# Softplus of a state space layer in two halves, with the work around it moved to other steps

## The reference

```python
xz = xs @ in_proj_w.T;  xin, z = split(xz)           # 768 channels each, L = 2304 positions
xin = silu(causal depthwise conv of xin, 4 taps)
dt, Bm, Cm = split(xin @ x_proj_w.T)                 # 24, 16, 16
dt = softplus(dt @ dt_proj_w.T + dt_proj_b)          # 768 step sizes for each position
h_t = exp(dt_t * A) * h_(t-1) + dt_t * B_t * x_t     # 16 states for each channel
y_t = sum over states of h_t * C_t
y = (y + xin * D) * silu(z);  out = layernorm(y @ out_proj_w.T)
```

## Time and profile before

| | |
|---|---|
| median of 3 runs | 5353.92 us (5347.02 to 5355.37) |
| profiled execution | 5347.93 us, span 5346.1 us |
| mean granted TensorE clock | 0.962 |
| busy share of the span | PE 88%, DVE 82%, ACT 57%, POOL 56% |

### The profile page before, as it was taken

The page is one execution under the profiler, slowest core; times in us unless marked ns, Lnnn a source line. Parts: engine busy times, 40 slices in busy tenths (PEclk is TensorE's granted clock), DMA queues, the critical chain, the costliest instruction groups (busy, mean ns, idle before and its releaser), DMA issues.

```text
span 5346.1 us, 78656 instructions
## 1 busy us (share of the span) xinstructions
PE 4686.3 (88%) x28623; PEld 3835.5 (72%) x28623; DVE 4381.3 (82%) x4965; ACT 3070.4 (57%) x6391; POOL 2970.7 (56%) x3552
## 2 busy tenths in 40 slices
PE   4888888888888888888888886779998899999999
PEld 2666666666666666666666665446877799999999
DVE  1999999999999999999999999677677765665555
ACT  3777777777777777777777774333332223333333
POOL 3776777777777777777777775456554520000000
PEclk8999999999999999999999999889797988999999
DMA  2001000001000001000000001110201021112110
GB/s 78 1 13 33 10 10 10 10 11 35 10 10 10 10 11 35 10 10 10 10 10 10 10 5 44 44 32 20 92 20 41 26 72 53 54 51 60 45 60 29
DMA packets 96933, 148.64 MB, mean 28 GB/s; under 512 B 5748, under 2 KB 93604, under 8 KB 96548
## 3 DMA queue, kind: packets, MB, share of 16 engines
q1 hardware_dynamic: 96548, 143.63, 8.4%
HBM read 101.00 MB, written 42.61 MB: 27 GB/s over the span
## 4 chain that ended last, share of the span: by engine, by line
PE 50%; issue 15%; DVE 15%; POOL 12%; ACT 7%; DMA 1%; POOLq 0%; DVEq 0%; SPq 0%; ACTq 0%
PE pw L1776 8%; PE pw L1763 6%; PE pw L462 6%; PE pw L451 6%; DVE a_h L744 5%; POOL a_dBT L882 4%; PE ps L413 3%; PE ps L353 3%; DVE b_cv L1393 3%; PE ps L373 2%; DVE a_acc L763 2%; PE ps L1763 2%; POOL a_xin L834 2%; POOL a_acc L894 2%; PE pw L1176 2%
## 5 line engine op out<-in xcount | busy, mean ns | idle before, releaser
L744 DVE TENSOR_TENSOR_SCAN a_h<-a_dA,pw 128x771 f32<-128x771 f32 x1152 | 2015.7, 1752 | 125.6 <-PE pw L451 124.6
L600 ACT ACTIVATE a_dA<-a_dt,a_Aneg 128x384 f32<-128x384 f32 x2304 | 1345.5, 607 | 155.0 <-DVE a_h L744 150.1
L462 PEld LDWEIGHTS pw<-g_ident,a_h 128*128 128x128 f32 x6912 | 786.6, 142 | 619.8 <-DVE a_acc L763 267.1
L882 POOL TENSOR_SCALAR a_dBT<-a_dtxT,a_BC 128x768 f32<-128x768 f32 x1152 | 1026.2, 909 | 300.7 <-PE pw L451 216.6
L462 PE MATMUL pw<-g_ident,a_h 128*128 128x128 f32 x6912 | 983.1, 279 | 227.5 <-DVE a_acc L763 158.1
L451 PE MATMUL pw<-g_ident,a_dBT 128*128 128x128 f32 x6912 | 958.9, 276 | 4.8 <-POOL a_dBT L882 4.8
L763 DVE SCALAR_TENSOR_TENSOR a_acc<-pw,a_BC,a_acc 128x768 f32<-128x768 f32 x912 | 915.3, 1004 | 52.5 <-PE pw L462 48.1
L451 PEld LDWEIGHTS pw<-g_ident,a_dBT 128*128 128x128 f32 x6912 | 806.5, 143 | 6.5 <-POOL a_dBT L882 5.5
L834 POOL TENSOR_TENSOR a_xin<-a_xin,a_tm 128x384 f32<-128x384 f32 x432 | 433.3, 1003 | 34.2 <-ACT a_tm L521 9.0
L1887 DVE TENSOR_TENSOR d_hf<-d_hf,d_wb 128x384 f32<-128x384 f32 x288 | 159.1, 557 | 312.4 <-ACT d_hf L1819 300.2
L894 POOL TENSOR_TENSOR a_acc<-a_acc,a_tm 128x768 f32<-128x768 f32 x168 | 307.4, 1830 | 171.1 <-ACT a_tm L614 170.2
(11 more groups left out here) (228 smaller groups left out, 9377.7 us busy)
## 6 DMA issues: line engine op xcount, KB each, us to landing
d_wb<-cw SPq DMA_DIRECT2D x24, 768.0 KB, 5.7
a_xs<-in_x SPq DMA_DIRECT2D x24, 576.0 KB, 3.9
x<-a_xs SPq DMA_DIRECT2D x24, 576.0 KB, 3.0
b_x<-x SPq DMA_DIRECT2D x24, 576.0 KB, 4.4
b_xs<-x SPq DMA_DIRECT2D x24, 576.0 KB, 5.0
e_xs<-x SPq DMA_DIRECT2D x24, 576.0 KB, 3.8
out<-e_xs SPq DMA_DIRECT2D x24, 576.0 KB, 5.8
a_sx<-in_x SPq DMA_DIRECT2D x54, 192.0 KB, 2.3
```

Of the source, the lines that this page charges most:

```text
L462: t = e.transpose(m["pw2"][:, c * 128:(c + 1) * 128], m[f"a_h{g % 2}"][:, c // 2, first_col(c) + tb * 128:first_col(c) + (tb + 1) * 128], ...
L600: e.activation(dA[:, first_col(c):first_col(c) + T], m[f"a_dt{k % 2}"][:, c, :], ACT.Exp, scale=m["a_Aneg"][:, c, n:n + 1]).then_inc(s["a_ ...
L744: e.tensor_tensor_scan(m[f"a_h{g % 2}"][:, p % 3, :], m[f"a_dA{pi % NDA}"][:], m[f"pw{pi % 2}"][:, COL:COL + PAIR], 1.0, ALU.mult, ALU.add ...
L882: t = e.tensor_scalar(m[f"a_dBT{g % 2}"][:, tb, :], m[f"a_dtxT{o}"][:, tb, :], m[f"a_BC{o}"][:, tb, n:n + 1], 1.0, ALU.mult, ALU.mult)
```

## The change

The softplus is taken in two halves of three channel tiles: ACT does V0 to V2, Exp and Ln of these, then V3 to V5, Exp and Ln of those, and POOL starts on the first three when their Ln is done. PE issues V3 to V5 two steps later, G2 two steps later, T0 to T5 some 3 to 5 steps earlier, and Z0 to Z5 0.6 to 5.7 steps later. The bank named by `V_BANK` is ps3 for all six, as before, so `pi` is `ps`.

```diff
@@ -310,9 +310,12 @@
 
 A_AT = (6.2, 8, 9.8, 11.6, 13.4, 15.2)
 O_AT, O_GAP, LN_AT = (18.8, 30, 40.2), (1.8, 1.6, 1.1), (29.5, 39.8, 47)
-G_AT = (60, 62.5, 66)
-T_AT = (78.6, 79.8, 81, 85.6, 86.6, 87.6)
-Z_AT = (63.5, 67.5, 71.5, 75, 82, 88.8)
+G_AT = (60, 62.5, 68)
+T_AT = (74, 75, 76, 82.4, 83.4, 84.4)
+V_BANK = "SSSSSS"
+SP_AT = (61, 66.5)
+DT_AT = (64.5, 66.5, 68.5, 70.5, 72.5, 74.5)
+Z_AT = (65.6, 69.6, 77.2, 79, 85.6, 89.4)
 
 LENT = (20, 22, 24, 26, 38, 41, 43)
 
@@ -387,7 +390,7 @@
         t = e.transpose(ps[:, tb * 32:tb * 32 + 32], m["a_tm0"][32:64, tb * 128:(tb + 1) * 128], ident[32:64, 32:64])
     t.then_inc(s["pe_BC"], 1)
     for i in range(6):
-        yield 58 + 0.8 * i
+        yield 58 + 0.8 * i + 2 * (i // 3)
         S.claim("a_v", 6 * k + i + 1)
         w.wait_ge("v_dt3", k + 1)
         w.wait_ge("v_w", 7)
@@ -537,23 +540,26 @@
     w.wait_ge("p_dbt", NS * (k - 1))
     e.activation(m[f"a_BC{o}"][:], ps[:, 0:96].rearrange("p (a n) -> p a n", n=32), ACT.Copy).then_inc(s["a_bc"], 1)
     dt = m[f"a_dt{o}"]
-    for i in range(6):
-        yield 58.4 + 0.8 * i
-        w.wait_ge("pe_V", 6 * k + i + 1)
-        w.wait_ge("p_cv", 24 * (k + 1))
-        if k % NQ < NQ - 1:
-            w.wait_ge("p_halo", k + 2)
-        w.wait_ge("p_dtx", 6 * (k - 1))
-        w.wait_ge("a_exp", 3 * PAIRS * (k - 1))
-        e.activation(dt[:, i, :], ps[:, 0:T], ACT.Abs, bias=pv[:, i, 5:6])
-        e.activation(raw[:, i, 3:T + 3], ps[:, 0:T], ACT.Relu, bias=pv[:, i, 5:6]).then_inc(s["a_v"], 1)
-    yield 64.5
-    w.wait_ge("a_v", 6 * (k + 1))
-    e.activation(dt[:], dt[:], ACT.Exp, scale=-1.0).then_inc(s["a_sp"], 1)
-    yield 67
-    w.wait_ge("a_sp", 2 * k + 1)
-    w.wait_ge("p_const", 3)
-    e.activation(dt[:], dt[:], ACT.Ln, bias=m["a_one"][:, 0:1]).then_inc(s["a_sp"], 1)
+    for hf in range(2):
+        for i in range(3 * hf, 3 * hf + 3):
+            yield 58.4 + 0.8 * i + (2 if hf else 0)
+            pi = ps if V_BANK[i] == "S" else pd
+            w.wait_ge("pe_V", 6 * k + i + 1)
+            w.wait_ge("p_cv", 24 * (k + 1))
+            if k % NQ < NQ - 1:
+                w.wait_ge("p_halo", k + 2)
+            w.wait_ge("p_dtx", 6 * (k - 1))
+            w.wait_ge("a_exp", 3 * PAIRS * (k - 1))
+            e.activation(dt[:, i, :], pi[:, 0:T], ACT.Abs, bias=pv[:, i, 5:6])
+            e.activation(raw[:, i, 3:T + 3], pi[:, 0:T], ACT.Relu, bias=pv[:, i, 5:6]).then_inc(s["a_v"], 1)
+        half = dt[:, 3 * hf:3 * hf + 3, :]
+        yield SP_AT[hf]
+        w.wait_ge("a_v", 6 * k + 3 * hf + 3)
+        e.activation(half, half, ACT.Exp, scale=-1.0).then_inc(s["a_sp"], 1)
+        yield SP_AT[hf] + 1
+        w.wait_ge("a_sp", 4 * k + 2 * hf + 1)
+        w.wait_ge("p_const", 3)
+        e.activation(half, half, ACT.Ln, bias=m["a_one"][:, 0:1]).then_inc(s["a_sp"], 1)
     for u in range(6):
         yield T_AT[u] + 0.4
         w.wait_ge("pe_T", 6 * k + u + 1)
@@ -836,10 +842,10 @@
     if k + 1 < NCH:
         halo_pool(e, m, w, k + 1)
     for i in range(6):
-        yield 69 + 2 * i
-        w.wait_ge("a_sp", 2 * k + 2)
+        yield DT_AT[i]
+        w.wait_ge("a_sp", 4 * k + 2 * (i // 3) + 2)
         e.tensor_tensor(dt[:, i, :], raw[:, i, 3:T + 3], dt[:, i, :], ALU.add).then_inc(s["p_dt"], 1)
-        yield 70 + 2 * i
+        yield DT_AT[i] + 1
         w.wait_ge("p_dt", 6 * k + i + 1)
         w.wait_ge("a_xi", k + 1)
         e.tensor_tensor(raw[:, i, 3:T + 3], dt[:, i, :], xin[:, i, :], ALU.mult).then_inc(s["p_dtx"], 1)
```

## The result

| | before | after |
|---|---|---|
| median | 5352.68 us (5347.02 to 5355.37, 4 runs) | 5396.91 us (5395.33 to 5398.17, 4 runs) |
| profiled execution | 5347.93 us | 5397.51 us |
| first scan starts | 126.1 us | 135.7 us |
| first scan to last scan | 3201.0 us | 3241.4 us |

The ratio is 1.0084, 95% interval 1.0066 to 1.0101: the change makes the kernel slower, by 44 us in the medians and 49.6 us between the two profiled executions. Of these 49.6, 40.4 lie between the first and the last scan and 9.6 ahead of the first; the rest of the kernel is as long as before.

What follows compares the result with a forecast made beforehand. DVE was taken to bound the first layer, so only its idle counts. Ordinary chunks 52, statistics chunks 10 and prologue 1.6 make 64 us; on the profiled 5347.9 that gives 5412, plus 6.0 for the median 5418; range 5365 to 5445.

Steps and rivals of the forecast that it cites:

- The V wait: Steps 63 to 65: V4 and V5 wait for V3's copies behind the half Exp and Ln; new DVE idle 1.0 us.
- Steps 81, 83, 85, 91: New DVE waits per ordinary chunk from moved T and Z pieces in PE's queue: 0.9, 1.2, 0.9 and 0.3 us.
- The rule of 3.25 us: Odd steps: DVE allows PE 3.25 us from one "turned" to the next, 1.37 already taken; any excess makes DVE idle.
- Step 83: Z3's last matmul, ACT's copy, then T3: PE ready after 4.68 us, DVE wants it after 3.44; 1.2 us wait.
- What goes: Four old waits vanish, at steps 63, 76, 85 and 90 (0.28, 0.24, 0.19, 1.10 us): 1.8 us a chunk.
- Sum for an ordinary chunk: New waits 4.4 us less 1.8 gone: +2.6 us for each of 20 ordinary chunks, +52.
- Chunks with statistics: Three chunks: DMA wait +2.6, T0 and T1 at step 76 -1.3, steps 79 to 90 +1.4, V +0.8; +3.5 each.
- TensorE's clock in ordinary chunks: Rival: PE's new pauses bring TensorE to 1.2 GHz in ordinary chunks, 3 us each, +60, 5475 us; chance 0.04.
- The prologue: Ahead of chunk 0, V3's copy waits for the half Exp and Ln instead of PE: +1.6 us.
- POOL and the split: POOL's earlier start costs and gives nothing; two more activations a chunk (0.3 us each) lie under ACT's idle.
- PE catches up between the steps (faster): Rival: PE catches up between steps 77 and 85, new waits don't come; 41 us less, 5313 us; chance 0.10.
- new and old waits cancel: Rival: one of three waits of steps 81 to 85 comes, others are absorbed; within 0.2%, 5354 us; chance 0.07.

Runs made afterwards that it cites:

- Z3 and T3 apart: Kernel after with Z3 due at 79.9 instead of 79 and T3 at 82.6 instead of 82.4: 5392.95 us in one run.
- Z5 late: Kernel before with only gate tile Z5 due at 89.4 instead of 88.8: 5320.33 us, ratio 0.9921.
- spread kernels: Three kernels from the kernel after, split kept, new due times for V, T, Z and gate groups: 5464.35, 5346.6 and 5345.94 us.
- v_together: Kernel after with V0 to V5 at their old steps and both halves of Exp and Ln behind V5: 5381.41 us, ratio to before 1.0043.
- second and third spread kernel: From the kernel after: second puts each gate group's three matmuls in one odd step, 5346.6 us; third moves all due times again, 5345.94 us.
- the split alone: Kernel before with Exp and Ln in two halves, both behind V5, every other piece at its old step: 5360.95 us, ratio 1.0008.
- gate early: Kernel before with only G0 to G2 at 57, 59 and 61 instead of 60, 62.5 and 66: 5322.0 us, ratio 0.9943.
- late first scan: Kernel before with a wait and five unused exps on ACT between V2's and V3's copies, ahead of chunk 0 only: 5359.55 us, ratio 0.9997.
- two edits together: Kernel before with Z5 at 89.4 and G0 to G2 at 57, 60 and 62.5: 5303.59 us, ratio 0.9895.
- first spread kernel: Kernel after with new spread due times, second and third gate matmul an odd step later than meant: 5464.35 us, ratio 1.0212.
- G2 back: Kernel after with only G2 at its old step, 66 instead of 68: 5386.62 us, ratio to before 1.0056.
- after again: Kernel after run once more, nothing edited: 5403.67 us in one run.

## Why the prediction was right, and where it was off

The forecast was 5418 us and the result 5396.91: right in sign and in the mechanism, 21 us too high. Between the scans I had 62 us and 40.4 came: 14 too many in the ordinary chunks, 5 in those with statistics, 13 at the steps 48 to 52, and 11 too few at step 68. The prologue had 8 too few, and the 6.0 that I added for the median over the profiled execution were not there in the kernel after (its median is 0.6 under it). That the total came within 21 us is in part luck, since misses of both signs met in it.

- **DVE bounds the layer, so only its idle time counts.** Held: 41.6 us more idle in the ledger for 40.4 us between the scans.
- **The V wait, 1.0 us.** Measured 0.79 in most chunks, 0.91 in the one shown, where the clock falls within "turned" (0.93 us in place of 0.82). The chain came out to a tenth: V4 3.95 us after the weighed predicted, 3.86 measured; V5 1.59 and 1.58; "turned" 0.28 and 0.29. The term was a little too large because DVE comes later than I had it, in the chunk shown 5.79 us after that weighed and not 5.65. The halves take 1.16 (Exp) and 1.25 us (Ln), where I took 1.20 and 1.30 from the rows. The Trainium skill (ScalarE: Activation LUTs, What ACT_TABLE_LOAD costs) has 186 ns and 0.833 ns for an element where scale and bias are immediate values, which makes an estimated 1.15 us for the Exp; the trace agrees with it to 0.02.
- **Steps 81, 83, 85, 91: 0.9, 1.2, 0.9 and 0.3.** Measured 0.89, 1.05, 0.88 and 0.19. The rule of 3.25 us between two "turned" stands where a piece waits for the bare copy of the one before, tested again by Z3 and T3 apart and by Z5 late; the spread kernels show where it falls short. Mis-sized was "Step 83": in the chunk shown PE had the scan of 84 ready 4.60 us after the "turned" of 81, not 4.68, and DVE came to it after 3.55, not 3.44.
- **What goes, 1.8 us.** Measured 1.92 (0.31, 0.24, 0.19, 0.08, 1.10).
- **Sum for an ordinary chunk, +2.6.** Measured 3.80 of new waits less 1.92, which is 1.88. The 0.7 too many are 0.2 at step 65, 0.15 at 83, and 0.1 each at 67, at 91 and in what goes; for 20 chunks 14 us.
- **Chunks with statistics, +3.5.** DVE idled 1.9 more (9.0 to 11.0). The +2.6 at the DMA was exact (4.08 to 6.65). The term "-1.3" for T0 and T1 at step 76 was too small: the wait ahead of scan 76 fell by 2.3, from 2.84 to 0.56. Together 5 us too many.
- **TensorE's clock in ordinary chunks.** I had this as a rival with 0.04 for 60 us (5418 + 60 is 5478, not the 5475 that stands there): "pauses of about 1 us are there now and leave 0.88". That step was wrong. Pauses of 1.70, 1.26 and 1.14 us, with a few groups of matmuls between them, brought the clock to 1.2 GHz in 8 of 23 chunks, for 11.1 us. When v_together took the V wait away, the slow matmuls went with it. The Trainium skill (TensorE: Matmul & The Clock Gate, Why this matters for your kernels) warns of long idle gaps between bursts of matmuls; here the clock fell behind gaps none of which was over 2 us, so the measurement goes further than that warning. By luck it was hidden by a miss of about the same size the other way: step 48, which I had as untouched, cost 9.2 us less, and steps 50 and 52 another 3.7.
- **The prologue, +1.6.** The profiled execution has 9.6. By the runs with the same prologue (first scan at 130.9 and 131.3) 4 to 5 of these are that execution's own. The rest is more than I had: three executions with the prologue of after average 132.6 and four with that of before 127.5. The half Exp and Ln ahead of V3, which the term was made of, can't be all of it, since v_together has them behind V5 and its first scan at 132.2. What the cause is stays open.
- **POOL and the split, nothing.** Held for the split: alone it gives 1.0008 with 1 inside the interval. POOL's earlier start has no run of its own, but in the kernel after DVE waits for POOL in one place alone, 0.3 us.
- **The range.** By its own terms (1.0 and 3.4 us a chunk in place of 2.6, 20 chunks) the inner range would be 5386 to 5434, not 5378 to 5440. The result lies in both.

Of the rivals, that PE catches up between the steps (faster) fell with the three waits in a row, none of them absorbed; that new and old waits cancel fell with them.

## What to carry to other kernels

Where one engine sets the pace and another, in-order one serves it between two fixed points, write down how much side work fits between them (here 3.25 us) and count each hand-over of a shared buffer against it (1.39 us from one piece to the next, for matmuls of 0.8); whatever goes over comes back every round, and a shift by one gap only moved it here. Count too what stands ahead of the copy in the order of the engine that copies (1.50 and 1.7 to 2.3 us a chunk in the second and third spread kernel). Look for the piece that stands ahead of a fixed point and could stand behind it: one due time from 88.8 to 89.4 gave 0.8% here, a bit over half of it by the wait that it was meant for. Where a store, a load and its use follow each other on one queue, move their start and not only their end: three pairs of steps earlier gave 0.6%, one pair later cost 2.5 us in each of its chunks.

## What the runs showed of the hardware

**The clock of TensorE is not the same from chunk to chunk for the same work.** Step 48 waits 2.00 us for ACT in every ordinary chunk, and behind that wait the clock falls in some and not in others. First the kernel before in two chunks, the second of which keeps its clock:

```profile
1121.51 0.91 PE L381 MATMUL ps<-a_xin,a_WxT 128*128 128x384 f32 x2 [2.00 <-ACT a_ob L490]
...
1123.29 1.49 PE L451 MATMUL pw<-g_ident,a_dBT 128*128 128x128 f32 x6
```

```profile
724.30 0.91 PE L381 MATMUL ps<-a_xin,a_WxT 128*128 128x384 f32 x2 [2.01 <-ACT a_ob L490]
...
725.70 0.82 PE L451 MATMUL pw<-g_ident,a_dBT 128*128 128x128 f32 x6
```

DVE idles 2.4 to 3.3 us there in the first kind and 1.59 in the second. The kernel before, the split alone, the gate early and the late first scan have 3 to 5 chunks of the cheap kind and 50.0 to 54.0 us at step 48; the kernel after, Z5 late and the two edits together have 10 or 11 and 42.7 to 44.1. In these three the long wait of step 90 is gone, but that is not the cause by itself: the first spread kernel has 1.11 us there and still 13 cheap chunks and 37.4 us at step 48. Why a chunk falls on one side is open; that the time of the chunk shifts the place at which the pause falls is a guess that nothing here tests.

**The start of the kernel differs from execution to execution.** A gate group of six matmul records takes 4.02 or 2.20 us. Some ahead of the first scan, in the profiled execution of after and then of before:

```profile
101.74 4.02 PE L416 MATMUL ps<-a_xn,a_WinT 128*128 128x384 f32 x6 [0.58 <-ACT a_sz L583]
...
127.12 2.20 PE L416 MATMUL ps<-a_xn,a_WinT 128*128 128x384 f32 x6 [0.58 <-ACT a_sz L583]
```

```profile
99.62 2.20 PE L413 MATMUL ps<-a_xn,a_WinT 128*128 128x384 f32 x6 [0.58 <-ACT a_sz L577]
```

Between 85 and 126 us the clock is at 1.2 GHz for most of the time in one, and in the other it rises ahead of 99.6. In the run with G2 back, whose instructions up to there are those of after, it is 2.20 us at 101.24, 3.88 at 107.41 and 2.20 again at 111.86. So 5 us of a kernel of 5350 are this.

**The layers that no edit touches vary too.** From the last scan to the end the profiled executions take from 2018.5 us (after) to 2029.6 (G2 back), 2018.9 in before and 2029.3 with the late first scan. Whether this comes with the program or with the execution is open. A difference of about 10 us between two single executions so says nothing of the first layer. Between the scans they can be compared more closely, but there too after and after again differ by 6.8 us.
